# Centred queries and their exponentials in two PSUM banks, and another order of VectorE's work in a group of rows

## The chip, the cores and the metric

The kernel runs on one core of a Trainium2 chip. The metric is the device time of one launch in microseconds (us), the median of the runs shown. The core has five engines that work in parallel and meet only through semaphores: TensorE (PE in the profile, with its weight loads as PEld), VectorE (DVE), ScalarE (ACT), GpSimd (POOL), and SyncE (SP), which only issues transfers. Two memories matter here: SBUF, which all engines reach, and PSUM, eight banks of 128 partitions x 512 floats, into which TensorE writes.

## The reference, cut to what matters

```python
x = x + 0.5 * ffn(layernorm(x))        # mixture of 8 experts, top 2, with a capacity
x = x + attn(layernorm(x))
x = x + 0.5 * ffn(layernorm(x))

def attn(x):                           # x: 4 batches x 2048 rows x 256, 16 heads of 16 columns
    q = split_heads(x @ Wq + bq)
    v = split_heads(x @ Wv + bv)
    q = softmax(q, axis=-1) * s        # over the 16 columns of a head
    k = softmax(q, axis=-2) * s        # over the 2048 rows of a batch
    ctx = einsum('bhnd,bhne->bhde', k, v)
    return merge(einsum('bhnd,bhde->bhne', q, ctx)) @ Wo + bo
```

The change concerns the attention alone, and there the first softmax: subtract the maximum of a head, take the exponential, sum, divide.

## The kernel before, in words

The 8192 rows lie in SBUF as 64 tiles of 128 rows (`xs`). The attention works on groups of four tiles (a "quad", 512 rows); a batch has four of them, so there are 16. Each engine runs one function `body(b, j)` for batch b and step j; the order of the work on an engine is the order in which its `body` is written, and nothing reorders it. `quads(b, j)` returns the quads that a step handles in its different stages. In step (b, j), with s = j + 1: `far` is quad s+3 (VectorE takes its statistics), `ahead` is s+2 (ScalarE normalizes it, GpSimd takes the low half, SyncE transposes it with a transfer), `turned` is s+1 (TensorE computes the queries), `now` is s (the softmax), `past` is s-1 (TensorE accumulates the keys' products), and `done` is s-5, of the batch before (TensorE multiplies the transposed queries by the batch's small matrix, and VectorE adds the result to `xs`). Steps with b = -1 only fill the pipeline; batch 0 has no `done`; batches 1 and 2 run in a hardware loop; batch 3 has three steps and no `far`.

One quad passes through these pieces, by their names and the lines before:

- VectorE `stats` (L1182 to L1189): mean and variance of the four tiles. The variances go to 32 columns of PSUM bank 1 (`mv`). It waits for the transfer that loads the tiles. For batches 0 and 1 each quad has its own load. For batches 2 and 3 there are four loads of 1 MB, issued one in each step of batch 0, and `stats` of the first quad of batch 2, which is `far` in step (1, 0), waits until all of them have landed (`at.x1_in`, 16 * 2 * QUADS).
- GpSimd `power` (L468, L470), ScalarE `norm_x` (L778) and `norm_hi` (L786), GpSimd `norm_low` (L474), SyncE `turn_x` (L598): the normalized rows as two half-precision halves, transposed. SyncE issues the 1 MB load (L585) right behind `turn_x` in the same step.
- TensorE `queries` (L1484, L1486): into bank 2 (two tiles) and bank 3 (two tiles). It waits for `at.cent`, which says that VectorE has read those banks for the quad before.
- VectorE `center`: two reductions for the maxima of the heads (L1213), then two subtractions (L1217), from banks 2 and 3 into `qb`, a float32 buffer of 128 x 1024 in SBUF (it lies in the memory of `gat`, and goes by that name in the profile).
- ScalarE `queries_exp` (L790): one exponential over 1024 columns, in place in `qb`.
- VectorE `sum_heads` (L1223) and `soften` (L1228, L1229): sums of the heads, reciprocal, and one product of 1024 columns, in place in `qb`.
- ScalarE `keys_exp` (L797, L798) and `queries_hi` (L804), GpSimd `keys_low` (L484) and `queries_low` (L479): they read the softened `qb`. GpSimd's last one counts up `at.qlo`, which frees `qb` for the quad two later.
- TensorE `keys` (L1496, L1500) and `finish` (L1516, into banks 6 and 7), VectorE `finish` (L1198).

In step j = 0 of batches 1 to 3 the small matrix of the batch before is made, in a chain that goes back and forth between TensorE (`m2_ctx` L1525, `m2_out` L1533, `m2_turn` L1538, `m2_spread` L1542), VectorE (`m2_sums`, `m2_ctx` L1234, `m2_out` L1240 and L1243, `m2_top` L1247, `m2_scale`, `m2_lo` L1256) and ScalarE (`m2_hi` L808). TensorE's next `finish` waits for its end. Behind the last attention step the second expert block begins; GpSimd's first instruction of it, L418, stands in its queue behind `queries_low` of the last quad.

Of the kernel before, what the change touches and what calls it, by code (L numbers as in the profile page):

```python
# [6 lines left out]
def macaron_block(nc, x, wq, bq, wv, bv, wo, bo, router_w, wg, wu, wd, out):  # L7
    f32, f16, b16, i32, u32 = (mybir.dt.float32, mybir.dt.float16, mybir.dt.bfloat16,
                               mybir.dt.int32, mybir.dt.uint32)
    ALU, ACT, AX = mybir.AluOpType, mybir.ActivationFunctionType, mybir.AxisListType  # L10
    add, sub, mult = ALU.add, ALU.subtract, ALU.mult
# [3 lines left out]
    B, SEQ, D = x.shape  # L15
# [6 lines left out]
    H = 16  # L22
    DH = D // H
    HS = float((DH ** 0.5) ** -0.25)
    QTOP = 2.0 ** 14
    BT = SEQ // P
    QUADS = BT // 4
# [11 lines left out]
    EPS = 1e-5  # L39
    XSCALE = 2.0 ** 10  # L40
    WTOP = 13
    LOOP_STEPS = 56
    HSHIFT = 2.0 ** -39
    ROUNDS = 15
    ONE = 1 << 23
# [7 lines left out]
    with ctx:  # L53
# [43 lines left out]
        rws = sb("rws", [P, 8], f32)  # L97
# [73 lines left out]
        qmax, qsum = v1[:, :], v3[:, :]  # L171
# [103 lines left out]
        def bc(ap, axis, n):  # L275

            ap = ap.unsqueeze(axis)
            shape = list(ap.shape)
            shape[axis] = n
            return ap.to_broadcast(shape)  # L280
# [5 lines left out]
        def wait_for(eng, sm, n):  # L286

            if not (isinstance(n, int) and n <= 0):
                eng.wait_ge(sm, n)
# [32 lines left out]
        def in_batches(b):  # L322

            return not isinstance(b, int) or 0 <= b < B
# [333 lines left out]
        def _(act):  # L658
# [127 lines left out]
                act.activation(at_rows[j][:, :, 0:D], xn[:, r, :, :], ACT.Copy).then_inc(at.hi, 1)  # L786

            def queries_exp(b, j):
                act.wait_ge(at.cent, QUADS * b + j + 1)
                act.activation(qb[:, j % 2], qb[:, j % 2], ACT.Exp, scale=rws[:, 7:8]).then_inc(at.ex, 1)  # L790

            def keys_exp(b, j):
                q, r = QUADS * b + j, j % 2
# [54 lines left out]
        def _(dve):  # L848
# [352 lines left out]
            def by_head(ap):  # L1201
                return ap.rearrange("p (h d) -> p h d", d=DH)

            def heads_of(j):
                return qb[:, j % 2].rearrange("p t (h d) -> p (t h) d", d=DH)

            def center(b, j):

                q, q3 = QUADS * b + j, heads_of(j)
                part = [slice(k * 2 * H, (k + 1) * 2 * H) for k in range(2)]  # L1210
                for k in range(2):
                    dve.wait_ge(at.q, 2 * q + k + 1)
                    ch.mark(dve.tensor_reduce(qmax[:, part[k]], by_head(bank[2 + k][:, :]), AX.X, ALU.max))  # L1213
                ch.wait()
                wait_for(dve, at.qlo, q - 1)
                for k in range(2):
                    i = dve.tensor_tensor(q3[:, part[k]], by_head(bank[2 + k][:, :]), bc(qmax[:, part[k]], 2, DH), sub)  # L1217
                i.then_inc(at.cent, 1)

            def sum_heads(b, j):  # L1220

                dve.wait_ge(at.ex, QUADS * b + j + 1)
                ch.step(dve.tensor_reduce(qsum, heads_of(j), AX.X, add))  # L1223

            def soften(b, j):

                q3 = heads_of(j)
                ch.step(dve.reciprocal(qsum, qsum))  # L1228
                dve.scalar_tensor_tensor(q3, q3, HS * QTOP, bc(qsum, 2, DH), mult, mult).then_inc(at.qs, 1)  # L1229


            def m2_ctx(m):
# [30 lines left out]
            def body(b, steps):  # L1263
                for j in steps:
                    far, _, _, now, _, done = quads(b, j)
                    m = b - 1 if in_batches(b - 1) else None
                    if now:
                        center(*now)
                    if m is not None and j == 0:
                        m2_sums(m)  # L1270
                        m2_ctx(m)
                        m2_out(m)
                    if far:
                        stats(*far)
                    if m is not None and j == 0:
                        m2_top(m)
                    if done and j == 1:
                        finish(done[0], 0)
                    if now:
                        sum_heads(*now)  # L1280
                    if m is not None and j == 0:
                        m2_scale(m)
                    if now:
                        soften(*now)
                    if m is not None and j == 0:
                        m2_lo(m)
                    if done and j:
                        finish(*done)

            def looped(b, steps):  # L1290
# [30 lines left out]
        def _(pe):  # L1321
# [153 lines left out]

            def queries(b, j, k):
                q = QUADS * b + j
                wait_for(pe, at.cent, q)
                if k == 0:
                    pe.wait_ge(xt_in[j % 2], turned_by((b, j)))  # L1480
                for t in range(2):
                    for n, (a, w) in enumerate(HALVES):
                        for d in range(KD):
                            i = pe.matmul(bank[2 + k][:, t * D:(t + 1) * D], at_xt[j % 2][:, 2 * k + t, a * KD + d, :],  # L1484
                                          wq16[:, w, d, :], start=(n == 0 and d == 0), stop=False)
                    i = pe.matmul(bank[2 + k][:, t * D:(t + 1) * D], bq_one[:, :], bq16[:, :], start=False, stop=True)  # L1486
                i.then_inc(at.q, 1)
# [95 lines left out]
            ffn(sems[0], 0, nothing)  # L1583
            attention_start()
            batches(pe, body)
            pe.wait_ge(at.cent, B * QUADS)
            attention_end(-1)
            ffn(sems[1], 3, attention_end)

# [22 lines left out]
```

## Time and profile before

| | us |
|---|---|
| median of 3 runs | 1919.36 |
| lowest and highest run | 1918.79 and 1923.34 |
| the profiled execution, by the clock of the other runs | 1917.76 |
| its span in the profile | 1916.0 |
| TensorE busy | 1616.2 |
| VectorE busy | 1246.2 |
| ScalarE busy | 887.6 |
| GpSimd busy | 874.8 |

The attention lies from about 857 to 1062 us of the span. The busy times are sums over the whole kernel, most of which is the two expert blocks, where TensorE is busy nearly all the time; they say little of the attention. There the timeline of each engine is read: each row has its start, the time that it took, the engine, the line, the operation, what is written and read, how many instructions are merged in the row, and in brackets how long the engine was idle before it and what released it.

### The profile page before, as it was taken

What the parts mean: (1) busy time and instruction counts of PE and PEld (TensorE: products, weight loads), DVE (VectorE), ACT (ScalarE), POOL (GpSimd) and SP (SyncE); (2) the same over time, 40 slices, a digit from 0 to 9 for tenths busy, and PEclk for the clock granted to TensorE, in tenths of its full rate; (3) what the DMA queues carried; (4) which work ended last, traced back from release to release, by engine and by line L of the source; (5) the groups of instructions that cost most, each with busy time, mean ns of one, the idle gap of its engine ahead of it and who ended that gap; (6) DMA issues with size and microseconds to landing.
All of it is one profiled execution on the core that took longest, in us unless ns stands there. A gap on an engine that the chain in (4) does not pass through costs nothing.

```text
span 1916.0 us, 40317 instructions
## 1 busy us (share of the span) xinstructions
PE 1616.2 (84%) x13943; PEld 1275.8 (67%) x13943; DVE 1246.2 (65%) x2883; ACT 887.6 (46%) x1627; POOL 874.8 (46%) x636
## 2 busy tenths in 40 slices
PE   4512899999999999995899751289999999999998
PEld 3411687877878787773577641168787787878876
DVE  8987748576574856526898897763745546465551
ACT  4511445445454444535665551144544545445452
POOL 5623262644536354235776652326264452635423
PEclk9999999999999999996999755589999999999999
DMA  6650461614425152226766450045161442515212
GB/s 214 212 185 14 108 122 30 145 41 107 78 70 126 37 132 52 31 29 165 154 146 146 137 195 4 14 108 116 36 145 44 104 83 65 128 42 126 58 25 28
DMA packets 261236, 182.16 MB, mean 95 GB/s; under 512 B 160938, under 2 KB 247860, under 8 KB 261172
## 3 DMA queue, kind: packets, MB, share of 16 engines
q1 hardware_dynamic: 230452, 139.37, 26.7%
q0 software_dynamic: 30720, 41.96, 13.2%
q8 instruction: 36, 0.59, 0.1%
q14 instruction: 28, 0.23, 0.0%
HBM read 89.01 MB, written 54.53 MB: 75 GB/s over the span
## 4 chain that ended last, share of the span: by engine, by line
PE 72%; DVE 12%; issue 6%; POOL 5%; DMA 2%; ACT 2%; DVEq 0%; SPq 0%; POOLq 0%; ACTq 0%
PE bank L1439 43%; PE bank L1452 22%; PE bank L1420 3%; POOL rstd L418 1%; POOL rows L422 1%; DVE kT L1020 1%; DVE rT L1020 1%; PE bank L1400 1%; DVE gat L1229 1%; PE bank L1484 1%; ACT xn L778 1%; DMA xs<-in_L_attn_x 1%; POOL gat L395 1%; DVE xn L937 1%; DVE v L1223 1%
## 5 line engine op out<-in xcount | busy, mean ns | idle before, releaser
L1439 PE MATMUL bank<-xT,w_g 128*128 128x320 f16 x3072 | 503.1, 300 | 30.9 <-DMA xT<-gat 30.9
L1095 DVE SCALAR_TENSOR_TENSOR unit_buf<-bank,sc_cur,unit_buf 128x320 f32<-128x320 f32 x512 | 281.5, 550 | 353.9 <-PE bank L1439 227.9
L1439 PE MATMUL bank<-xT,w_u 128*128 128x320 f16 x3072 | 502.5, 300 | 0.0
L720 ACT ACTIVATE unit_buf<-bank,sc_cur 128x320 f32<-128x320 f32 x512 | 269.5, 526 | 407.1 <-PE bank L1439 405.6
L1452 PE MATMUL bank<-w_d,xs 128*128 128x256 f16 x3840 | 423.8, 273 | 0.0
L1452 PEld LDWEIGHTS bank<-w_d,xs 128*128 128x128 f16 x3840 | 375.2, 98 | 44.4
L1439 PEld LDWEIGHTS bank<-xT,w_g 128*128 128x128 f16 x3072 | 295.7, 99 | 141.0 <-issue 30.6
L389 POOL TENSOR_TENSOR hot_v<-hot_b,val 128x400 bf16<-128x400 bf16 x128 | 147.7, 1154 | 519.9 <-DVE hot_b L1078 519.9
L1439 PEld LDWEIGHTS bank<-xT,w_u 128*128 128x128 f16 x3072 | 301.3, 98 | 117.7
L1101 DVE TENSOR_TENSOR xs<-unit_buf,xs 128x320 f16<-128x320 f32 x512 | 268.0, 523 | 2.2
L395 POOL DMA_INDIRECT gat<-rows_d,id_next x160 | 177.0, 1106 | 200.4 <-DVE id_next L1088 140.0
L726 ACT ACTIVATE xs<-unit_buf 128x320 f16<-128x320 f32 x512 | 235.8, 461 | 10.4 <-DVE unit_buf L1095 10.4
L745 ACT ACTIVATE xs<-bank,w_fac 128x256 f32<-128x256 f32 x160 | 76.0, 475 | 277.4 <-PE bank L1452 276.3
L408 POOL DMA_INDIRECT out_x<-xs,id_cur x80 | 143.0, 1788 | 84.6 <-issue 76.1
L408 POOL DMA_INDIRECT x_d<-xs,id_cur x80 | 142.6, 1782 | 84.0 <-issue 73.6
L915 DVE SCALAR_TENSOR_TENSOR w_g<-raw_gu,sc_next,w_g 128x1024 f16<-128x1024 f32 x32 | 41.1, 1284 | 93.2 <-ACT w_g L661 93.2
L1420 PEld LDWEIGHTS bank<-hot_v,hot_a 128*128 128x128 bf16 x1024 | 82.3, 161 | 28.5 <-DVE hot_a L1080 24.3
L1420 PE MATMUL bank<-hot_v,hot_a 128*128 128x50 bf16 x1024 | 80.6, 219 | 22.2 <-POOL hot_v L389 22.2
L1400 PE MATMUL bank<-cnt,same_e 128*128 128x3 f32 x60 | 17.6, 363 | 95.7 <-DVE rT L1020 95.7
L422 POOL TENSOR_TENSOR rows<-xn,rows 128x1024 f16<-128x1024 f32 x32 | 68.4, 2136 | 45.2 <-ACT rows L667 45.2
L1080 DVE TENSOR_TENSOR hot_a<-pos_a,slot_a 128x1024 bf16<-128x1024 bf16 x128 | 87.3, 682 | 0.0
L1400 PEld LDWEIGHTS bank<-cnt,same_e 128*128 128x128 f32 x60 | 15.0, 310 | 98.9 <-DVE rT L1020 98.9
(229 smaller groups left out, 1815.2 us busy)
## 6 DMA issues: line engine op xcount, KB each, us to landing
rows_d<-rows SPq DMA_DIRECT2D x32, 512.0 KB, 3.4
raw_gu<-in_L_ffn_wg SPq DMA_DIRECT2D x16, 1024.0 KB, 6.3
raw_gu<-in_L_ffn_wu SPq DMA_DIRECT2D x16, 1024.0 KB, 9.3
raw_d<-in_L_ffn_wd SPq DMA_DIRECT2D x16, 1024.0 KB, 5.5
x_d<-xs SPq DMA_DIRECT2D x1, 8192.0 KB, 32.6
out_x<-xs SPq DMA_DIRECT2D x16, 512.0 KB, 3.7
xs<-in_L_attn_x SPq DMA_DIRECT2D x7, 1024.0 KB, 5.6
xs<-x_d SPq DMA_DIRECT2D x5, 1024.0 KB, 6.1
```

The source lines that it names most:

```text
L389: pool.tensor_tensor(hot_v[:, r], bc(hot_b[:, r], 2, 5), bc(vv, 3, ST), mult).then_inc(S.hot_v_ready, 1)
L395: pool.indirect_dma_start(out=gat[:, s, :], out_offset=None, in_=rows_d, in_offset=bass.IndirectOffsetOnAxis(ap=id_next[:, s:s + 1], axis= ...
L408: pool.indirect_dma_start(out=dst, out_offset=bass.IndirectOffsetOnAxis(ap=id_cur[:, s:s + 1], axis=0), in_=stage[:, s, :], in_offset=None ...
L422: pool.tensor_tensor(rows[:, r, :, D:2 * D], xn[:, r, :, :], rows[:, r, :, 0:D], sub).then_inc(S.lo_ready, 1)
L720: act.activation(act_s[:, u % 2, :], bank[u % 2][:, 0:CW], ACT.Silu, scale=sc_cur[:, 3:4]).then_inc(S.s_ready, 1)
L726: act.activation(hid[:, 0, f, c * CW:(c + 1) * CW], h32[:, u % HB, :], ACT.Copy).then_inc(S.hhi_ready, 1)
L1080: dve.tensor_tensor(hot_a[:, r], bc(pa, 1, P), slot_a[:, :, :], ALU.is_equal).then_inc(S.hot_a_ready, 1)
L1095: dve.scalar_tensor_tensor(h32[:, u % HB, :], bank[2 + u % 2][:, 0:CW], sc_cur[:, 4:5], act_s[:, u % 2, :], mult, mult).then_inc(S.h32_rea ...
L1101: dve.tensor_tensor(hid[:, 1, f, c * CW:(c + 1) * CW], h32[:, u % HB, :], hid[:, 0, f, c * CW:(c + 1) * CW], sub).then_inc(S.h_ready, 1)
L1420: last = pe.matmul(bank[6][:, 0:5 * ST], hot_a[:, i % 2, :, t], hot_v[:, i % 2, t].rearrange("p v s -> p (v s)"), start=(i == 0 and t == 0 ...
L1439: mm = pe.matmul(bank[2 * m + u % 2][:, 0:CW], wgu[m][:, w, k, f * P:(f + 1) * P], xT[:, a * KD + k, c * CW:(c + 1) * CW], start=(j == 0 a ...
L1452: mm = pe.matmul(bank[4 + s % 2][:, 0:D], hid[:, a, f, s * P:(s + 1) * P], wdn[:, w, f, :], start=(f == 0 and j == 0), stop=(f == FT - 1 a ...
```

## The change

`center` now writes its differences into PSUM banks 0 and 1 (which the attention did not use otherwise, but for the 32 columns of `mv` in bank 1), the exponential runs there in place, in two instructions of 512 columns, the sums of the heads are taken from there in two, and `soften` reads the banks and writes `qb` in two. The wait for `at.qlo` moves from `center` to `soften`. `at.cent` and `at.ex` count two per quad, and `queries` waits for each of its banks alone. In VectorE's `body`, `stats` moves ahead of `center`, and `finish` of steps j > 1 moves from the end of the step to the place between `center` and `sum_heads`.

```diff
             def queries_exp(b, j):
-                act.wait_ge(at.cent, QUADS * b + j + 1)
-                act.activation(qb[:, j % 2], qb[:, j % 2], ACT.Exp, scale=rws[:, 7:8]).then_inc(at.ex, 1)
+                q = QUADS * b + j
+                for k in range(2):
+                    act.wait_ge(at.cent, 2 * q + k + 1)
+                    act.activation(bank[k][:, :], bank[k][:, :], ACT.Exp, scale=rws[:, 7:8]).then_inc(at.ex, 1)
...
             def center(b, j):
...
                 ch.wait()
+                for k in range(2):
+                    dve.tensor_tensor(by_head(bank[k][:, :]), by_head(bank[2 + k][:, :]), bc(qmax[:, part[k]], 2, DH),
+                                      sub).then_inc(at.cent, 1)
+
+            def sum_heads(b, j):
+
+                q = QUADS * b + j
+                for k in range(2):
+                    dve.wait_ge(at.ex, 2 * q + k + 1)
+                    ch.mark(dve.tensor_reduce(qsum[:, part[k]], by_head(bank[k][:, :]), AX.X, add))
+                ch.wait()
+
+            def soften(b, j):
+
+                q = QUADS * b + j
+                ch.step(dve.reciprocal(qsum, qsum))
                 wait_for(dve, at.qlo, q - 1)
                 for k in range(2):
-                    i = dve.tensor_tensor(q3[:, part[k]], by_head(bank[2 + k][:, :]), bc(qmax[:, part[k]], 2, DH), sub)
-                i.then_inc(at.cent, 1)
-
-            def sum_heads(b, j):
-
-                dve.wait_ge(at.ex, QUADS * b + j + 1)
-                ch.step(dve.tensor_reduce(qsum, heads_of(j), AX.X, add))
-
-            def soften(b, j):
-
-                q3 = heads_of(j)
-                ch.step(dve.reciprocal(qsum, qsum))
-                dve.scalar_tensor_tensor(q3, q3, HS * QTOP, bc(qsum, 2, DH), mult, mult).then_inc(at.qs, 1)
+                    last = dve.scalar_tensor_tensor(by_head(qb[:, j % 2, 2 * k:2 * k + 2].rearrange("p t d -> p (t d)")),
+                                                    by_head(bank[k][:, :]), HS * QTOP, bc(qsum[:, part[k]], 2, DH),
+                                                    mult, mult)
+                last.then_inc(at.qs, 1)
...
                     m = b - 1 if in_batches(b - 1) else None
+                    if far:
+                        stats(*far)
                     if now:
                         center(*now)
                     if m is not None and j == 0:
                         m2_sums(m)
                         m2_ctx(m)
                         m2_out(m)
-                    if far:
-                        stats(*far)
+                    if done and j > 1:
+                        finish(*done)
                     if m is not None and j == 0:
                         m2_top(m)
                     if done and j == 1:
...
                         m2_lo(m)
-                    if done and j:
+                    if done and j == 1:
                         finish(*done)
...
             def queries(b, j, k):
                 q = QUADS * b + j
-                wait_for(pe, at.cent, q)
+                wait_for(pe, at.cent, 2 * q - 1 + k)
```

The first place is VectorE's queue at step (1, 0), behind the branch into the loop (L299). In the rows `v` stands for the small buffers of maxima and sums, `gat` for `qb`, `bst` for the statistics, `zr`, `wT`, `t` and `mx` for pieces of the small matrix. Before:

```order
L299 UNCONDITIONAL_BRANCH
L1213 TENSOR_REDUCE v<-bank 128x32 [waits at_q]
L1217 TENSOR_TENSOR gat<-bank,v 128x512 [waits at_qlo,at_dstep]
L1260 RECIPROCAL zr<-bank 128x2 [waits at_gt]
L1234 TENSOR_TENSOR wT<-bank,same_h 128x256 [waits at_ctx]
L1240 SCALAR_TENSOR_TENSOR t<-bank,zr,rT 128x256 [waits at_a]
L1243 TENSOR_REDUCE mx<-t 128x1 [waits at_dstep]
L289 ISA [waits at_x1_in]
L1182 BN_STATS bst<-xs 128x6
L1247 TENSOR_REDUCE m_top_s<-bank 1x1 [waits at_m_max]
L1223 TENSOR_REDUCE v<-gat 128x64 [waits at_ex]
```

The same place now; L1184 is `stats`, L1216 the subtraction, L1224 the sums.

```order
L299 UNCONDITIONAL_BRANCH
L289 ISA [waits at_x1_in]
L1184 BN_STATS bst<-xs 128x6
L1213 TENSOR_REDUCE v<-bank 128x32 [waits at_q]
L1216 TENSOR_TENSOR bank<-bank,v 128x512 [waits at_dstep]
L1267 RECIPROCAL zr<-bank 128x2 [waits at_gt]
L1241 TENSOR_TENSOR wT<-bank,same_h 128x256 [waits at_ctx]
L1247 SCALAR_TENSOR_TENSOR t<-bank,zr,rT 128x256 [waits at_a]
L1250 TENSOR_REDUCE mx<-t 128x1 [waits at_dstep]
L1254 TENSOR_REDUCE m_top_s<-bank 1x1 [waits at_m_max]
L1224 TENSOR_REDUCE v<-bank 128x32 [waits at_ex] x2
```

The statistics, and with them the wait for the loads (`at_x1_in`), have moved from behind `m2_out` to the head of the step, ahead of the centring and of the whole chain for the small matrix.

The second place is VectorE's queue in step j = 2 of the loop; L1198 (now L1200) is `finish`. Before:

```order
L1223 TENSOR_REDUCE v<-gat 128x64 [waits at_ex]
L1228 RECIPROCAL v<-v 128x64 [waits at_dstep]
L1229 SCALAR_TENSOR_TENSOR gat<-gat,v 128x1024 [waits at_dstep]
L1198 ISA [waits at_out]
L1198 SCALAR_TENSOR_TENSOR xs<-bank,mx,xs 128x512
```

And now, from the subtraction on:

```order
L1216 TENSOR_TENSOR bank<-bank,v 128x512
L1197 ISA
L1200 ISA [waits at_out]
L1200 SCALAR_TENSOR_TENSOR xs<-bank,mx,xs 128x512
L1224 TENSOR_REDUCE v<-bank 128x32 [waits at_ex] x2
L1230 RECIPROCAL v<-v 128x64 [waits at_dstep]
L1233 SCALAR_TENSOR_TENSOR gat<-bank,v 128x512 [waits at_qlo,at_dstep]
```

The additions to `xs`, which wait for TensorE's product (`at_out`), have moved ahead of the sums and of the softening.

## Rows read from the trace of the kernel before

**Rows 1.** By stretch: length, busy PE, PEld, DVE, ACT, POOL (count), PEclk, DMA share, GB/s.
```profile
922.77:932.99 10.22, 7.37 (x57) 4.61 (x53) 8.55 (x18) 6.90 (x9) 8.49 (x6) 0.83 1.05 208
948.25:993.01 44.76, 41.15 (x383) 31.96 (x384) 41.32 (x90) 28.92 (x39) 33.01 (x20) 1.00 0.68 144
```
**Rows 2.** Timeline of VectorE, one step of batch 0: start, duration, then the instruction.
```profile
912.56 1.27 DVE L1213 TENSOR_REDUCE v<-bank 128x32 f32<-128x512 f32 x2
913.87 1.29 DVE L1217 TENSOR_TENSOR gat<-bank,v 128x512 f32<-128x512 f32 x2
915.07 1.39 DVE L1182 BATCH_NORM_STATS2 bst<-xs 128x6 f32<-128x256 f32 x4
...
918.65 1.22 DVE L1223 TENSOR_REDUCE v<-gat 128x64 f32<-128x1024 f32 x1 [1.38 <-ACT gat L790]
...
920.49 2.35 DVE L1229 SCALAR_TENSOR_TENSOR gat<-gat,v 128x1024 f32<-128x1024 f32 x1
```
**Rows 3.** Timeline of ScalarE, the same step.
```profile
912.67 1.06 ACT L797 ACTIVATE xT<-gat 128x1024 f32<-128x1024 f32 x1 [3.32 <-DVE gat L1229]
...
915.52 2.06 ACT L778 ACTIVATE xn<-xs,nmean,rstd 128x256 f32<-128x256 f32 x4
917.49 1.13 ACT L790 ACTIVATE gat<-gat,rws 128x1024 f32<-128x1024 f32 x1
```
**Rows 4.** Timelines of GpSimd and VectorE, where L1229 and GpSimd meet and where not.
```profile
919.64 2.13 POOL L474 TENSOR_TENSOR rows<-xn,rows 128x1024 f16<-128x1024 f32 x1 [0.67 <-ACT rows L786]
921.73 1.99 POOL L468 TENSOR_TENSOR rstd<-rstd,mhalf 128x4 f32<-128x4 f32 x1
...
943.75 1.01 POOL L468 TENSOR_TENSOR rstd<-rstd,mhalf 128x4 f32<-128x4 f32 x1
946.22 1.23 DVE L1229 SCALAR_TENSOR_TENSOR gat<-gat,v 128x1024 f32<-128x1024 f32 x1
```
**Rows 5.** Groups by line, VectorE, 892 to 1036 us: count | busy, mean ns | idle.
```profile
L1217 DVE TENSOR_TENSOR gat<-bank,v 128x512 f32<-128x512 f32 x26 | 16.7, 686 | 0.4
L1198 DVE SCALAR_TENSOR_TENSOR xs<-bank,mx,xs 128x512 f32 x16 | 11.2, 738 | 0.2
```
**Rows 6.** Timelines of ScalarE, SyncE and VectorE around the last load of batches 2 and 3.
```profile
927.70 1.13 ACT L790 ACTIVATE gat<-gat,rws 128x1024 f32<-128x1024 f32 x1
934.09 1.05 SPq L585 DMA_DIRECT2D xs<-x_d  x1
941.18 1.40 DVE L1182 BATCH_NORM_STATS2 bst<-xs 128x6 f32 x4
```
**Rows 7.** Columns as in rows 1: the two microseconds in which the transfers end.
```profile
939.00:940.00 1.00, 1.00 (x8) 0.78 (x8) 0.33 (x1) 1.00 (x3) 0.84 (x1) 1.00 0.48 169
940.00:941.00 1.00, 1.00 (x10) 0.59 (x7) 0.97 (x3) 1.00 (x2) 0.00 (x0) 1.00 0.00 0
```
**Rows 8.** Timeline of TensorE, first `finish` behind step (1, 0).
```profile
948.25 2.79 PE L1516 MATMUL bank<-kT,raw_gu 128*128 128x256 f16 x24 [1.14 <-DVE kT L1256]
```
**Rows 9.** Chain that ended last, step (3, 0), without statistics: start, duration, what.
```profile
1027.75 1.13 PE bank L1533 x4
...
1035.53 0.75 DVE kT L1256
```
**Rows 10.** Timeline of TensorE: queries after a long idle time, and without one.
```profile
878.66 1.46 PE L1484 MATMUL bank<-wq,xt 128*128 128x256 f16 x6 [15.90 <-DMA xt<-rows]
...
950.87 0.82 PE L1484 MATMUL bank<-wq,w_u 128*128 128x256 f16 x6
```
**Rows 11.** Timelines of TensorE, VectorE and GpSimd at the end of the attention.
```profile
1048.49 2.78 PE L1516 MATMUL bank<-kT,raw_gu 128*128 128x256 f16 x24
...
1046.45 1.28 DVE L1213 TENSOR_REDUCE v<-bank 128x32 f32<-128x512 f32 x2
...
1052.11 1.23 DVE L1229 SCALAR_TENSOR_TENSOR gat<-gat,v 128x1024 f32<-128x1024 f32 x1
...
1059.62 1.98 POOL L418 TENSOR_TENSOR rstd<-rstd,mhalf 128x4 f32<-128x4 f32 x2
```

More of the change, by code:

```diff
@@ L41, in macaron_block @@
     WTOP = 13
-    LOOP_STEPS = 56
+    LOOP_STEPS = 60
     HSHIFT = 2.0 ** -39
@@ L1202, in by_head @@
                 return ap.rearrange("p (h d) -> p h d", d=DH)
-            def heads_of(j):
-                return qb[:, j % 2].rearrange("p t (h d) -> p (t h) d", d=DH)
+            part = [slice(k * 2 * H, (k + 1) * 2 * H) for k in range(2)]
             def center(b, j):
-                q, q3 = QUADS * b + j, heads_of(j)
-                part = [slice(k * 2 * H, (k + 1) * 2 * H) for k in range(2)]
+                q = QUADS * b + j
                 for k in range(2):
@@ L1214, in center @@
                 ch.wait()
+                for k in range(2):
[8 more added lines that the diff above has]
+            def soften(b, j):
+                q = QUADS * b + j
+                ch.step(dve.reciprocal(qsum, qsum))
                 wait_for(dve, at.qlo, q - 1)
                 for k in range(2):
-                    i = dve.tensor_tensor(q3[:, part[k]], by_head(bank[2 + k][:, :]), bc(qmax[:, part[k]], 2, DH), sub)
-                i.then_inc(at.cent, 1)
-            def sum_heads(b, j):
-                dve.wait_ge(at.ex, QUADS * b + j + 1)
-                ch.step(dve.tensor_reduce(qsum, heads_of(j), AX.X, add))
-            def soften(b, j):
-                q3 = heads_of(j)
-                ch.step(dve.reciprocal(qsum, qsum))
-                dve.scalar_tensor_tensor(q3, q3, HS * QTOP, bc(qsum, 2, DH), mult, mult).then_inc(at.qs, 1)
+                    last = dve.scalar_tensor_tensor(by_head(qb[:, j % 2, 2 * k:2 * k + 2].rearrange("p t d -> p (t d)")),
+                                                    by_head(bank[k][:, :]), HS * QTOP, bc(qsum[:, part[k]], 2, DH),
+                                                    mult, mult)
+                last.then_inc(at.qs, 1)
             def m2_ctx(m):
@@ L1585, in _ @@
             batches(pe, body)
-            pe.wait_ge(at.cent, B * QUADS)
+            pe.wait_ge(at.cent, 2 * B * QUADS)
             attention_end(-1)
```

## The prediction, made before the changed kernel ran

> **What bounds the kernel now.** I read the page first: TensorE is busy for most of the span, but in the expert blocks, which the change doesn't touch. So the question is what sets the pace in the attention, from 857 to 1062 us, and the view for it is the busy time by stretch, then the timelines of single engines there. The reader is to see two regimes. In batch 0 a step takes 10.2 us and no engine is full: TensorE 7.4, VectorE 8.6, ScalarE 6.9, GpSimd 8.5 [rows 1]. Such a pace is set by a ring of waits. From batch 1 on a batch of four steps takes 44.76 us, with TensorE busy for 41.15 and VectorE for 41.32: there the two are nearly full, and a cut in waiting can bring 3.6 us a batch at most [rows 1].
>
> The ring of batch 0 reads off two timelines. ScalarE's L797 starts when VectorE's L1229 has ended (it waited 3.32 us for it); from its start at 912.67 ScalarE goes without a gap through L797, L798, L804 and L778 to the exponential, which starts at 917.49 and ends at 918.62 [rows 3]. VectorE, idle for 1.38 us, starts the sums at 918.65, and L1229 at 920.49; it ends at 922.84, which frees ScalarE again [rows 2]. Around: 4.82 to the exponential, 1.13 in it, 1.84 for sums and reciprocal, 2.35 for L1229, some 0.07 of hand-over: 10.21.
>
> L1229 takes 1.23 us where GpSimd isn't at work on SBUF, and 2.35 in the ring; there GpSimd's L474 runs from 919.64 to 921.77, and 921.77 plus 1.1 is just where L1229 ends. The other way round GpSimd's tiny L468 takes 1.99 beside L1229 and 1.01 away from it [rows 2, 4]. Both are one at a time: each costs the other about 1 us. VectorE's L1217 and L1198, with one operand in PSUM and one large or small one in SBUF, keep their means of 686 and 738 ns over 892 to 1036 us, though GpSimd works most of that time [rows 1, 5].
>
> [...]
>
> **The change, part by part.**
>
> *The ring in batch 0.* The product reads PSUM. I take 2 x 0.67 = 1.35 us for its two halves, between L1217 and L1198, which have its form [rows 5]; bounds 1.25 and 1.5. The two exponentials of 512 columns: L790 takes 1.13 for 1024, so a half has about 0.43 of columns and 0.2 to 0.25 of fixed time; both take 1.2 to 1.3 [rows 3]. No row has an activation that reads and writes PSUM; at worst 0.1 more each. But VectorE starts its first sum after the first half, so behind the second only a half sum, 0.64, stands, and the reciprocal, 0.6. The new ring: 4.82 + 1.3 + 0.7 + 0.6 + 1.35 + 0.03 = 8.8 us, against 10.21. VectorE needs for itself 2.05 (statistics, with their waits) + 2.56 (centring, L1213 and L1217 [rows 2]) + 1.3 + 0.55 + 1.35 = 7.8, and GpSimd, rid of its own 1 us, 7.6. The transfers are the tight resource: 1.05 of 10.22 us in the row of the last step [rows 1], with overlaps counted twice. I let them take 0.3 us back in all. In the first quad the 2.05 us of statistics no longer stand between centring and sums, but in idle time ahead of the queries; the exponentials' 1.3 and their hand-overs remain there, and I estimate 0.45 from it. Four turns of the ring lie between the exponential of quad 0 and that of quad 4: 4 x 1.41 + 0.45 - 0.3 = **-5.8 us** (bounds -3.1, if transfers hold a step at 9.55, and -7.2).
>
> [...] The rows show 1.27 for two reductions of 512 from PSUM against 1.22 for one of 1024 from SBUF, 0.05 apart; my sum goes by these.
>
> *The wait for the last load.* In step (1, 0), `stats` needs the last 1 MB load of batches 2 and 3. SyncE issues it at 934.09, 5.3 us after the end of the exponential of quad 4 (928.83), behind the transposition that follows that exponential. Transfers still run to the middle of 939 to 940 and then stop; so the load lands near 940.1, 11.3 us after the exponential [rows 6, 7]. Before, VectorE softened, centred and made the small matrix first, came to `stats` at 941.18 and didn't wait. Now `stats` is first. VectorE has softened 2.6 us after the exponential and stands there for 8.7 us. Behind it in its queue are the centring (TensorE's next queries wait for that), the sums, and the chain for the small matrix, for which `finish` waits. From the landing: stats 2.05, centring 2.56, masked product 0.85, 0.1 to TensorE's `m2_out`. From there to the end of L1256 the rows of step (3, 0), where VectorE has no statistics in between, as now, give 1036.28 - 1027.75 = 8.5 us; 0.2 more for the halves, 8.7 [rows 9]. Then TensorE's clock: it is idle for some 8 us ahead of this. After an idle time of 15.9 us it worked at 1.2 instead of 2.4 GHz (six matmuls in 1.46 instead of 0.82 us) [rows 10]. I take 2.2 us, bounds 0 and 5. Sum: 11.3 + 2.05 + 2.56 + 0.85 + 0.1 + 8.7 + 2.2 = 27.8 us from the exponential to the first `finish`, against 948.25 - 928.83 = 19.4 before [rows 6, 8]: **+8.4 us** (bounds +5.5 and +12).
>
> *Batches 1 and 2.* L1229 no longer stretches, and `finish` covers the exponential. VectorE's own order, all starts added: step j = 1 10.5, j = 2 and 3 9.2 each, then stats, centring and masked product 5.5, and 8.7: 43.1 us with hand-overs, against 44.76. **-1.65 us.** From `finish` of batch 1 to that of batch 2 there are no stats in the last step, but TensorE's products of the keys end only then; I count -0.9 there. Together -2.55 (bounds 0, if TensorE sets the pace with its waits, and -5, if both batches come down to 42.3).
>
> *The end.* In the last step VectorE centres from 1046.45 to 1049.05; `finish` now stands ahead of the sums, and TensorE ends that product only at 1048.49 + 2.78 = 1051.27. So VectorE waits for TensorE: 1052.0 behind `finish`, then 1.3 + 0.55 + 1.35 = 1055.2, where L1229 ended at 1053.34 before. Behind it are ScalarE's and GpSimd's last pieces, and GpSimd's L418, which opened the second expert block at 1059.62 [rows 11]. **+1.8 us** (bounds 0 and 2.6).
>
> The wait moved to `soften` is for quad q-2 and long fulfilled. The column range of `mv` in bank 1 meets no instruction of another engine. `queries` gets bank 2 some 0.6 us earlier, hidden. The rest of the kernel is the same.
>
> Sum: -5.8 + 8.4 - 2.55 + 1.8 = +1.85 us. The profiled execution took 1917.76 (span 1916.0), so 1919.6 there. The median of the runs shown is 1.6 higher, 1919.36, so **1921.2 us**.
>
> **The rivals.**
>
> *The load isn't missed.* If it lands by the time VectorE comes to it, or with little wait (the sooner transposition and a load that needs fewer than 6 us would do it), the path from exponential to `finish` is bound by TensorE's keys and `m2_ctx`, and comes to about 18.5 us instead of 27.8: 0.9 below the 19.4. The sum is then -5.8 - 0.9 - 2.55 + 1.8 = -7.5: **1911.9 us**, faster. For it: the load's landing is inferred from the transfers' activity, not shown. Against it: 5.3 us to the issue are the same chain as before, and VectorE arrives at 2.6.
>
> *VectorE waits for TensorE in each `finish`.* By my schedule VectorE reaches `finish` in steps 2 and 3 about 15.0 and 24.2 us behind the first one, and TensorE has its products at 14.8 and 24.3. There is no slack. It decides when TensorE is more than 0.2 us later, as behind a late transposition or at the low clock; then each of the four steps loses what TensorE is late, say 1.2, and the saving of the two batches turns into a loss: +4.8 over my sum, **1926.0 us**, slower. Against it: TensorE has 3.6 us of idle time a batch to catch up in [rows 1].
>
> *The contention stays.* If an input in PSUM doesn't free the product from GpSimd, about 1.1 us return in each of 8 steps, and GpSimd keeps its 1.99: +9, **1930 us**. Against it stands L1217 [rows 5].
>
> **How the numbers follow.** Forecast 0.62, load not missed 0.15, `finish` waits 0.17, contention stays 0.06. The forecast's own range is 1916 to 1926. Taking in most of the first two rivals, the range is 1913 to 1928. A change of this kernel can be told from none beyond 0.3%, 5.8 us: faster means below 1913.6, slower above 1925.1. The forecast gives some 0.08 of its chance to slower and 0.02 to faster; the first rival is mostly faster, the second and third mostly slower: faster 0.15, same 0.62, slower 0.23.
>
> **What would show it.** Right, if: in batch 0 a step takes 8.7 to 9.1 us; the product's halves take 0.65 to 0.7 us each beside GpSimd's L474, and L468 takes 1.01; in step (1, 0) VectorE is idle for 7 to 10 us ahead of its first statistics, released by a transfer, and TensorE works at a lower clock right behind; the two batches take 42 to 43.5 us each; and VectorE's last `finish` waits some 2 us for TensorE. Wrong, if that idle time is under 3 us, if batch 0 keeps 10.2 us a step, or if VectorE waits for TensorE in every `finish` of the loop.

## The result, and the profile after

| | before | after |
|---|---|---|
| median of 6 runs each, us | 1919.45 | 1928.51 |
| lowest to highest | 1918.79 to 1923.34 | 1928.01 to 1929.17 |
| ratio, 95% interval | | 1.0043 (1.0033 to 1.0054) |
| profiled execution, its span | 1917.76, 1916.0 | 1928.49, 1926.8 |

The changed kernel is slower by 9.1 us. The forecast was 1921.2, with a range of 1913 to 1928: the median lies 0.5 us above the range's upper end, and the case that came true, slower, had 0.23. The ratio is that of the two kernels' runs with its interval; the medians of the table give 1.0047.

The attention can be measured by itself, from VectorE's write of `same_h` (859.88 before, 859.97 after) to GpSimd's L418 (1059.62 [rows 11], and 1068.67). It took 199.74 us before and takes 208.70 after: 8.96 more, nearly the whole difference of the medians. The landmarks between are the end of the exponential of quad 4 and TensorE's first `finish` product of each batch.

| stretch, us | before | after | change | predicted |
|---|---|---|---|---|
| to the exponential of quad 4 | 68.95 | 63.02 | -5.9 | -5.8 |
| from there to the first finish | 19.42 | 29.12 | +9.7 | +8.4 |
| batch 1, finish to finish | 44.76 | 47.18 | +2.4 | -1.65 |
| batch 2 | 43.32 | 43.81 | +0.5 | -0.9 |
| to L418 | 23.29 | 25.57 | +2.3 | +1.8 |

**The ring.** VectorE's timeline of one step of batch 0 after the change (start, duration, instruction), which answers to [rows 2]:

```profile
893.77 1.30 DVE L1216 TENSOR_TENSOR bank<-bank,v 128x512 f32<-128x512 f32 x2
895.94 1.29 DVE L1224 TENSOR_REDUCE v<-bank 128x32 f32<-128x512 f32 x2 [0.87 <-ACT bank L792]
897.26 0.55 DVE L1230 RECIPROCAL v<-v 128x64 f32<-128x64 f32 x1
897.85 1.29 DVE L1233 SCALAR_TENSOR_TENSOR gat<-bank,v 128x512 f32<-128x512 f32 x2
```

And GpSimd's, beside it, for [rows 4]:

```profile
897.54 2.13 POOL L474 TENSOR_TENSOR w_g<-xn,w_g 128x1024 f16<-128x1024 f32 x1 [0.80 <-ACT w_g L786]
899.62 1.01 POOL L468 TENSOR_TENSOR rstd<-rstd,mhalf 128x4 f32<-128x4 f32 x1
```

L1233's two halves take 1.29 together in the middle of L474, where one instruction took 2.35, and L468 is back at 1.01. Of the four steps between the exponentials of quads 0 and 4 three take 8.7 us and one 9.1.

**The load.** VectorE and SyncE in step (1, 0), which answer to [rows 6]:

```profile
924.37 1.29 DVE L1233 SCALAR_TENSOR_TENSOR gat<-bank,v 128x512 f32<-128x512 f32 x2
936.34 1.40 DVE L1184 BATCH_NORM_STATS2 bst<-xs 128x6 f32 x4 [10.68 <-DMA xs<-x_d]
```

```profile
923.42 4.61 SPq L607 DMA_TRANSPOSE raw_gu<-unit_buf  x1
928.21 2.02 SPq L598 DMA_TRANSPOSE xt<-w_g  x1
930.27 0.89 SPq L585 DMA_DIRECT2D xs<-x_d  x1
```

VectorE stands for 10.68 us. The load is issued 7.3 us after the exponential (its end is 922.99) instead of 5.3, because SyncE needs 4.61 us for the transposition ahead of it, L607, for which it needed 1.95 before:

```profile
929.33 1.95 SPq L607 DMA_TRANSPOSE raw_gu<-unit_buf  x1
```

It comes back in split_again and ahead_end, below, with 4.51 and 4.40 us at the same place. Behind the wait TensorE's timeline:

```profile
941.82 2.07 PE L1542 MATMUL bank<-wo,wT 128*128 128x256 f32 x4 [10.03 <-DVE wT L1241]
943.68 1.49 PE L1493 MATMUL bank<-wq,xt 128*128 128x256 f16 x6
...
952.11 2.79 PE L1525 MATMUL bank<-kT,raw_gu 128*128 128x256 f16 x24 [0.41 <-DVE kT L1263]
956.07 0.83 PE L1493 MATMUL bank<-wq,w_u 128*128 128x256 f16 x6 [1.17 <-DVE bank L1216]
```

It worked at the lower level, 1.2 GHz, right behind 10 us of idling (the granted clock is 0.50 from 940 to 944 us): six matmuls in 1.49 us, in 0.83 later.

**The batches.** The last row shows the first of two surprises, in step 1. Before, VectorE centred right behind the end of the small matrix, and TensorE had the free banks when its first `finish` product was done. Now the statistics stand between them, and TensorE waits 1.17 us. Step 1 has two `finish`es, that of quad 0 ahead of the sums and that of quad 1 at its end; VectorE waits in both halves of the second, and the step takes 11.8 us from centring to centring (954.00 to 965.80), where the prediction counted 10.5:

```profile
961.71 0.75 DVE L1200 SCALAR_TENSOR_TENSOR xs<-bank,mx,xs 128x512 f32 x1 [0.69 <-PE bank L1525]
963.02 0.75 DVE L1200 SCALAR_TENSOR_TENSOR xs<-bank,mx,xs 128x512 f32 x1 [0.56 <-PE bank L1525]
```

The second surprise stands in step (2, 0). First VectorE, then GpSimd, then TensorE:

```profile
986.60 0.16 DVE L1267 RECIPROCAL zr<-bank 128x2 f32<-128x2 f32 x1
986.80 1.81 DVE L1268 TENSOR_SCALAR zr<-zr 128x2 f32<-128x2 f32 x1
```

```profile
986.46 2.12 POOL L479 TENSOR_TENSOR unit_buf<-gat,unit_buf 128x1024 f16<-128x1024 f32 x1 [0.18 <-ACT unit_buf L806]
```

```profile
989.07 1.50 PE L1542 MATMUL bank<-wo,wT 128*128 128x256 f32 x4 [2.34 <-DVE wT L1241]
990.36 1.48 PE L1493 MATMUL bank<-wq,xt 128*128 128x256 f16 x6
```

L1268 scales two numbers per partition, from SBUF to SBUF. It ends at 988.61, L479 at 988.58: it took until GpSimd's instruction was done. TensorE's idle time ahead of `m2_out` is 2.34 us, against 0.66 in the same step before, and behind it the clock is low again for a while (0.61 from 989 to 992 us). The two stretches after, for [rows 1] (columns as there):

```profile
952.11:999.29 47.18, 42.48 (x383) 32.48 (x384) 40.74 (x98) 29.48 (x43) 30.06 (x20) 0.96 0.65 134
999.29:1043.10 43.81, 40.93 (x384) 31.92 (x385) 38.39 (x88) 29.43 (x43) 28.91 (x18) 1.00 0.64 141
```

**The end.** VectorE waits for TensorE in the last early `finish`, as [rows 11] had it coming, by 1.04 and 0.92 us:

```profile
1056.87 0.75 DVE L1200 SCALAR_TENSOR_TENSOR xs<-bank,mx,xs 128x512 f32<-128x512 f32 x1 [1.04 <-PE bank L1525]
1058.54 0.75 DVE L1200 SCALAR_TENSOR_TENSOR xs<-bank,mx,xs 128x512 f32<-128x512 f32 x1 [0.92 <-PE bank L1525]
...
1061.11 1.29 DVE L1233 SCALAR_TENSOR_TENSOR gat<-bank,v 128x512 f32<-128x512 f32 x2
```

### The profile page after: what moved, and what is told of

Its sections match the earlier page's. It is cut to its first block, busy times and chain, and to the rows that moved or that the text cites. A ratio compares the mean times of both kernels' runs of the same rounds, so it can differ in the third digit from the quotient of the medians.

```text
span 1926.8 us, 40369 instructions
## 1 busy us (share of the span) xinstructions
PE 1614.3 (84%) x13943; PEld 1274.2 (66%) x13943; DVE 1242.0 (64%) x2915; ACT 889.2 (46%) x1643; POOL 864.2 (45%) x636
## 3 DMA queue, kind: packets, MB, share of 16 engines
q0 software_dynamic: 30720, 41.96, 13.3%
## 4 chain that ended last, share of the span: by engine, by line
PE 75%; DVE 10%; issue 5%; POOL 4%; DMA 3%; ACT 1%; SPq 1%; DVEq 0%; POOLq 0%; ACTq 0%
PE bank L1448 43%; PE bank L1461 22%; PE bank L1429 3%; PE bank L1493 2%; PE bank L1525 1%; POOL rstd L418 1%; PE bank L1505 1%; DVE kT L1022 1%; DVE rT L1022 1%; POOL rows L422 1%; PE bank L1409 1%; DMA xs<-in_L_attn_x 1%; DVE xn L939 1%; PE bank L1495 1%; POOL hot_v L389 1%
## 5 line engine op out<-in xcount | busy, mean ns | idle before, releaser
L395 POOL DMA_INDIRECT gat<-rows_d,id_next x160 | 180.9, 1130 | 200.4 <-DVE id_next L1090 140.0
L408 POOL DMA_INDIRECT out_x<-xs,id_cur x80 | 138.9, 1737 | 84.6 <-issue 76.1
```

The source lines that it names most:

```text
L395: pool.indirect_dma_start(out=gat[:, s, :], out_offset=None, in_=rows_d, in_offset=bass.IndirectOffsetOnAxis(ap=id_next[:, s:s + 1], axis= ...
L408: pool.indirect_dma_start(out=dst, out_offset=bass.IndirectOffsetOnAxis(ap=id_cur[:, s:s + 1], axis=0), in_=stage[:, s, :], in_offset=None ...
```

## The experiments

All runs in one table. Stretches in us, each from one trace, "first finish" from the write of `same_h`, the others as above; "ratio" compares the run with before on the same chip, and can differ by up to 0.0014 from the quotient of the medians. split_wait, stats_back, psum_only and order_only ran on a chip on which before takes 2008.57 us (the block ahead of the attention is some 40 us slower there). The three of these with the PSUM banks have ratios 0.0034 to 0.0051 below those of their near twins split_again, back_odd and move_odd. The attention of stats_back and psum_only is within 1 us of their twins', and split_wait's is even 4.3 us longer than split_again's. Why is open, since before has no trace on that chip; the text below leans on their stretches alone.

| kernel | first finish | batch 1 | batch 2 | end | attention | ratio (95%) |
|---|---|---|---|---|---|---|
| before | 88.37 | 44.76 | 43.32 | 23.29 | 199.7 | 1 |
| before_again | 88.59 | 45.46 | 44.71 | 23.29 | 202.1 | |
| after | 92.14 | 47.18 | 43.81 | 25.57 | 208.7 | 1.0043 (1.0033, 1.0054) |
| split_wait | 84.64 | 48.21 | 43.79 | 25.23 | 201.9 | 0.9938 (0.9917, 0.9960) |
| split_again | 83.77 | 44.76 | 43.79 | 25.24 | 197.6 | 0.9989 (0.9980, 0.9997) |
| stats_back | 87.86 | 47.27 | 47.23 | 25.60 | 208.0 | 1.0010 (0.9995, 1.0025) |
| back_odd | 89.20 | 47.28 | 47.25 | 25.24 | 209.0 | 1.0044 (1.0031, 1.0057) |
| psum_only | 87.70 | 45.52 | 42.45 | 22.37 | 198.0 | 0.9942 (0.9925, 0.9958) |
| move_odd | 87.48 | 45.46 | 42.44 | 22.36 | 197.7 | 0.9988 (0.9980, 0.9997) |
| order_only | 96.07 | 50.64 | 45.76 | 25.10 | 217.6 | 1.0098 (1.0081, 1.0116) |
| ahead_end | 81.68 | 47.09 | 43.79 | 22.37 | 194.9 | 0.9975 (0.9967, 0.9984) |
| ahead_end_zr | 84.95 | 44.77 | 43.80 | 22.37 | 195.9 | 0.9965 (0.9952, 0.9977) |
| best | 82.54 | 44.16 | 43.44 | 22.36 | 192.5 | 0.9948 (0.9935, 0.9961) |
| sbuf_best | 89.98 | 52.28 | 47.54 | 23.28 | 213.1 | 1.0054 (1.0040, 1.0067) |

before_again is before once more, for its trace:

> The kernel before, unchanged, for its trace on the same chip as the variants. I measure the attention's length from VectorE's write of same_h to GpSimd's L418 of the second expert block: 199.7 us in the first trace of before. If the attention doesn't depend on the chip it is 199.2 to 200.2 here, and all differences of whole runs between variants beyond their attention's lengths are noise of the expert blocks; if this chip's transfers are slower, it is above 203, and the variants' gains over before are larger here than on the first chip.

Its attention came out 2.3 us longer than in the first trace, above what I expected. In steps (2, 0) and (3, 0) TensorE's matmuls fell into the lower clock (`m2_out` took 1.82 and 2.08 us instead of 1.12 and 1.13), and 2.1 of the 2.3 us lie in the two batches that end there. So 2 us between two single traces of the attention is noise, and a smaller difference needs the ratio or the row that makes it.

**The wait for the loads.** split_wait, and the same kernel again as split_again:

```diff
-                elif j == 0:
-                    dve.wait_ge(at.x1_in, 16 * 2 * QUADS)
+                elif j % 2 == 0:
+                    dve.wait_ge(at.x1_in, 16 * (QUADS + 1 + j // 2) + 32 * (b - 2))
```

> The changed kernel, but the statistics of a quad of batches 2 and 3 wait only for the load that holds that quad, not for all four. Theory (the wait for the last load costs most of the loss): VectorE no longer waits in step (1, 0), and TensorE's first finish comes 9 to 11 us sooner, bound by the keys and m2_ctx (exponential of quad 4 to finish about 18.5 us instead of 29); everything behind keeps its pace, 47 and 44 us for the two batches. Total 1928.5 - 10 = 1918.5 us (1917 to 1920.5). Rival (other engines give it back, because transfers or TensorE are just as late): less than 3 us of gain, 1926 or more.

> The same kernel as split_wait (the changed kernel, with VectorE's statistics waiting for their own load alone), on a chip where the kernel before takes the 1919 us of the first trace, since on the other chip transfers and expert blocks took longer. Theory A (the wait for all loads is worth 6 to 8 us): no idle time of VectorE ahead of the statistics in step (1, 0), the first finish at 82 to 85 us instead of 92.1, batches as in the changed kernel (47.2 and 43.8) and the end too, so the attention is 200 to 203 us long and the run 6 to 8 us below the changed kernel's 1928.5: 1920.5 to 1922.5. Theory B (VectorE then waits for something else there, for the low clock's matmuls or for TensorE): the first finish above 88, the run above 1925.

VectorE no longer idles there, and the first `finish` comes at 83.8 us instead of 92.1: 8.4 us for the wait. It is one trace; the other kernels with the same banks, order up to there and own-load wait (split_wait, ahead_end, ahead_end_zr, best) have it at 81.7 to 85.0, so the wait is worth 7 to 10 us. split_again's median is 1917.82, 10.7 below after's, more than expected, since L1268 this time met no GpSimd instruction in batch 1. Its rows, and the stretch of that batch:

```profile
978.71 0.17 DVE L1268 TENSOR_SCALAR zr<-zr 128x2 f32<-128x2 f32 x1
1021.74 1.25 DVE L1268 TENSOR_SCALAR zr<-zr 128x2 f32<-128x2 f32 x1
```

```profile
944.02:988.78 44.76, 41.07 (x383) 31.83 (x384) 39.22 (x98) 29.49 (x43) 30.07 (x20) 1.00 0.70 142
```

In the table batch 1 takes 44.8 us where L1268 took 0.17 and 47.1 to 48.2 where it took 1.49 or 1.81 (after, ahead_end, split_wait), all with the same order in that batch's steps 0 and 1. In batch 2 the stretch costs nothing: L1268 took 1.25 or 1.26 us in after, split_wait and split_again and 0.24 in ahead_end, and the batch takes 43.8 us in all four. There TensorE's product ends only behind L1268, and VectorE waits for it in any case: 0.46 us more in after, 1.47 in ahead_end.

**The order's two parts, undone one by one.** In stats_back and psum_only the statistics stand behind the small matrix again. Mean and variance can't then lie in bank 1, where the exponentials are, so they went to a small buffer in SBUF:

```diff
-                    ch.mark(dve.bn_aggr(mv[:, r, g, :], bst[:, r, g, :]))
+                    ch.mark(dve.bn_aggr(at_mv[:, r, g, :], bst[:, r, g, :]))
...
-                dve.tensor_scalar(nmean[:, r, :], mv[:, r, :, 0], -1.0, None, mult)
+                dve.tensor_scalar(nmean[:, r, :], at_mv[:, r, :, 0], -1.0, None, mult)
```

> The changed kernel with the statistics back in their old place, behind m2_out; since bank 1 is in use there, mean and variance go to a small SBUF buffer instead. Theory (statistics ahead of the centring cost the load wait, and in the loop hold back TensorE's queries in step 1 and the small matrix in step 0): the load wait is gone (-10), the two batches take about 43.5 and 42.5 us instead of 47.1 and 43.9 (-5): 1913.5 us (1911 to 1916). Rival (the loop is slow for another reason, the stretched L1268 and TensorE waits in finish): batches stay at 46 to 47 and 44, 1918 to 1919. If the two small operations on the new SBUF buffer get into the way of GpSimd, they take 1 to 2 us instead of 0.16 in many steps and the total is up to 8 us more.

> Only the move to PSUM: all of VectorE's work in the order of before, mean and variance in a small SBUF buffer as in stats_back. Theory: finish ahead of the sums isn't needed where the statistics cover the exponential, and it costs about 2 us at the end of the attention, so this is 0 to 3 us faster than stats_back: 1911.5 us (1909 to 1915). Batch 0 keeps its 8.8 us a step. Rival (the early finish helps, as cover): slower than stats_back by 1 us or more.

> Only VectorE's new order (statistics first, finish in the middle for j > 1), with the centred queries in SBUF as before. Theory (the order loses, PSUM wins): batch 0 keeps 10.2 us a step, in step (1, 0) VectorE waits 6 to 9 us for the load, and the loop loses too: 1919.4 + 8 + 5 + 2 = 1934 us (1930 to 1938). Rival (the move to PSUM is what costs): about 1919 to 1922 us.

order_only shows the reorder without the move: 17.8 us more attention, with a wait of 7.42 us for the load. The other two missed what was expected of them: the wait for the load is gone in both, but stats_back's batches take 47.3 and 47.2 us instead of 43.5 and 42.5, and psum_only's attention is only 1.7 us shorter than before's. They were confounded by that buffer (L1191, `nmean` from it, takes up to 2.03 us), so they were run again with five columns in it instead of four:

> The move to PSUM with the order of before, and mean and variance in SBUF with five columns instead of four (one of padding), so that VectorE's two small instructions on them have an odd width. Theory A: what stretched those instructions to 0.65 to 1.96 us in psum_only is that VectorE takes a fast mode for an even number of elements from SBUF to SBUF and must wait for GpSimd there. Then with five columns each takes 0.16 us, the steps of batch 0 take 8.7 to 8.9 us instead of 9.5, a batch takes 42.8 to 43.3 us instead of 45.5 (1.14 + 0.49 + 0.48 + 0.55 less), and the attention 187 to 191 us against 198.0. Theory B: any VectorE instruction from SBUF to SBUF waits, whatever its width; then all stays as in psum_only, 197 to 199.

> The same, but with finish of steps j > 1 between the centring and the sums, as in the changed kernel. Theory A (the early finish is what costs the batches): VectorE comes to it before TensorE has the product, waits there 1 to 2.5 us in each of those steps and holds up the sums behind it: batches longer than move_odd's by 1.5 to 2.5 us each, the end by 2 to 2.5 us, the attention 6 to 9 us longer than in move_odd. Theory B (only the place of the statistics costs the batches): the attention is at most 2.5 us longer than in move_odd, all of it at the end.

Theory A of move_odd fell: the odd width changes nothing. A group of VectorE's instructions by form, 880 to 1060 us, and one of them with GpSimd's instruction beside it:

```profile
L1192 DVE TENSOR_SCALAR nmean<-at_mv 128x5 f32<-128x5 f32 x13 | 15.3, 1177 | 0.4
```

```profile
897.86 1.96 DVE L1192 TENSOR_SCALAR nmean<-at_mv 128x5 f32<-128x5 f32 x1
899.73 0.16 DVE L1193 TENSOR_SCALAR rstd<-at_mv 128x5 f32<-128x5 f32 x1
```

```profile
897.67 2.12 POOL L480 TENSOR_TENSOR unit_buf<-gat,unit_buf 128x1024 f16<-128x1024 f32 x1
```

L1192 ends at 899.82, L480 at 899.79. Read from PSUM the same operation takes 0.16. With that cost in it, the move with the old order still gives 0.9988, and `finish` made early on top of it 1.0044: 11.2 us more attention, of which 2.9 are the end, 6.6 the two batches, and the rest lies ahead of the first `finish`, where the two kernels are the same. In back_odd's step 3 L1192 takes 1.96 us (0.64 in move_odd) and the scaling behind it 1.64 (0.31), TensorE idles 3.0 us in both batches and falls to the lower clock. I put the batches' length down to that chain, and not to a wait in `finish`, since VectorE doesn't wait for TensorE in the loop's `finish` there at all; no run has the early `finish` with that buffer and without the stretch. Theory A had the cost but not its place.

ahead_end is split_again with `finish` of every step back at the step's end:

```diff
-                    if done and j > 1:
-                        finish(*done)
...
-                    if done and j == 1:
+                    if done and j:
                         finish(*done)
```

> split_wait (the changed kernel with statistics waiting for their own load alone) with finish of all steps put back at the end of the step; the statistics stay ahead of the centring. Against split_wait's 201.9 us. Theory A (both parts of the order cost): the end gets back 2 to 2.5 us and the steps 2 and 3 of the batches some 0.5 us each, but step 1 keeps TensorE waiting for the centring (1.2 us of TensorE idle ahead of the queries, VectorE 1.2 us late in finish): 196 to 199 us, still 4 or more above move_odd. Theory B (only the early finish costs): within 1.5 us of move_odd.

The end comes down from 25.24 to 22.37, and batch 2 stays at 43.79; batch 1 is 2.3 us longer, which is L1268 again (1.49 us here, 0.17 in split_again). With the statistics ahead, the early `finish` costs 2.9 us, at the end alone. The run is 4.2 us below before.

**L1268.** ahead_end_zr scales first, from PSUM, and takes the reciprocal in SBUF:

```diff
-                ch.step(dve.reciprocal(zr[:, :], bank[5][:, 0:KD]))
-                ch.mark(dve.tensor_scalar(zr[:, :], zr[:, :], HS, None, mult))
+                ch.step(dve.tensor_scalar(zr[:, :], bank[5][:, 0:KD], 1.0 / HS, None, mult))
+                ch.mark(dve.reciprocal(zr[:, :], zr[:, :]))
```

> ahead_end with the scaling of the sums' reciprocal in another order: the tensor_scalar reads PSUM (bank 5, times 1/HS) and the reciprocal of 128 x 2 then runs in SBUF. Theory A (a tensor_scalar with input and output in SBUF waits for GpSimd's instruction, one from PSUM doesn't, and a reciprocal doesn't): L1267 and L1268 take 0.16 to 0.17 us each in every batch, where L1268 took 1.49; TensorE waits 1.2 us less for the masked product and keeps its clock; batch 1 gets 1.3 to 2.5 us shorter (47.1 to 44.6 to 45.8), batch 2 stays at 43.8, the run 1912.5 to 1914. Theory B (what is stretched is whichever small instruction stands there): the new instruction from PSUM takes 1.4 us and nothing changes, 1915.

All eight instructions take 0.15 to 0.17 us, and batch 1 takes 44.77 us instead of 47.09. In that batch no GpSimd instruction happened to run at that place. In batch 2 GpSimd's L484 ran over both, and they still took 0.16 and 0.17; in batch 1 it is best, below, that has one there. VectorE and GpSimd in best:

```profile
976.76 0.15 DVE L1267 TENSOR_SCALAR zr<-bank 128x2 f32<-128x2 f32 x1
976.95 0.17 DVE L1268 RECIPROCAL zr<-zr 128x2 f32<-128x2 f32 x1
```

```profile
976.06 2.12 POOL L479 TENSOR_TENSOR unit_buf<-gat,unit_buf 128x1024 f16<-128x1024 f32 x1 [0.93 <-ACT unit_buf L806]
```

The median of ahead_end_zr fell by 1.4 us, inside the two intervals; the attention doesn't show it as a whole, because the first `finish` came 3.3 us later (TensorE waited 2.68 us for transposed rows instead of 1.46, and VectorE then for it).

**Step 1.** best puts the statistics of step j = 1 behind its softening:

```diff
-                    if far:
+                    if far and j != 1:
                         stats(*far)
...
+                    if far and j == 1:
+                        stats(*far)
                     if done and j:
```

> ahead_end_zr, with the statistics of step j = 1 put behind that step's softening, so that the centring, which frees TensorE's banks, comes first behind m2_lo there. Theory A (the centring behind the statistics is what holds TensorE in step 1): TensorE doesn't wait 1.17 us for L1216 behind its first finish, VectorE doesn't wait 0.7 and 0.55 us for the second finish, and each of the batches 1 and 2 gets 1.2 to 2 us shorter: 42.3 to 43.5 each, the run 1909 to 1912. Theory B (the time comes back, because ScalarE now waits for those statistics in step 2 and its exponentials come late): the batches stay within 0.5 us of ahead_end_zr's.

TensorE goes from `finish` to the queries without a gap. The gain is 0.6 and 0.35 us in the batches, half or less of what I expected at the least: VectorE now idles 0.93 us ahead of the sums, and TensorE 0.8 us one step later, as Theory B had it in part. best takes 1910.19 us, 9.8 below before on its chip and 18.3 below the changed kernel.

**The move alone, under the best order.** sbuf_best is best with queries and exponentials in SBUF again, as in before:

> The order, the wait and the scaling of best, with queries and exponentials in SBUF as in the kernel before. It says what the PSUM banks are worth by themselves. Theory A (the move frees VectorE's product and GpSimd from each other, and this is a gain of its own): the steps of batch 0 take 10.2 us again instead of 8.7, which alone is 5.9 us to the fourth exponential, and in the batches the product takes 2.35 us in some steps: each 0.5 to 2 us longer; the attention 199 to 203 us against best's 192.5, the run 1917 to 1921. Theory B (the order gives the gain, and the product's contention is hidden in it): the run within 2 us of best's 1910.2.

It takes 1931.03, 20.8 us more than best, twice what Theory A said. VectorE's timeline in a step of batch 1, and GpSimd's:

```profile
968.47 1.22 DVE L1223 TENSOR_REDUCE v<-gat 128x64 f32<-128x1024 f32 x1 [1.22 <-ACT gat L790]
969.73 0.55 DVE L1228 RECIPROCAL v<-v 128x64 f32<-128x64 f32 x1
970.32 2.36 DVE L1229 SCALAR_TENSOR_TENSOR gat<-gat,v 128x1024 f32<-128x1024 f32 x1
```

```profile
969.47 2.12 POOL L474 TENSOR_TENSOR rows<-xn,rows 128x1024 f16<-128x1024 f32 x1 [3.10 <-ACT rows L786]
971.55 1.99 POOL L468 TENSOR_TENSOR rstd<-rstd,mhalf 128x4 f32<-128x4 f32 x1
```

In SBUF the order of before is the better one: sbuf_best has 13.3 us more attention than before, though it also has the loads' own wait and the other scaling. In steps 1 to 3 of batch 1 VectorE idles 1.43, 1.22 and 1.21 us ahead of the sums, where the statistics of before's order left 0, 0.49 and 0; TensorE idles 2.83 us for the centring of step 2 and 2.88 us ahead of `m2_out`, and its clock is low behind that. L1229 takes 2.36 us in steps 1 to 3, in before 1.65 and twice 2.36.

In PSUM no run shows which order is better. best has 5.2 us less attention than move_odd, but 4.9 of these lie ahead of the first `finish`, where move_odd's L1192 takes 1.96 us and its steps 9.5 instead of 8.7; the two batches take 87.6 us in best and 87.9 in move_odd. The old order in PSUM, with mean and variance out of the way of GpSimd, was not run.

## Why the prediction was right or wrong

- **The ring, -5.8:** right in size and cause. Steps of 8.8 us were forecast and 8.7 measured, but for one of 9.1, and the halves take 0.65 us each. The sum reads rows 1 loosely in one place: their 1.05 is a share of the time and not microseconds.
- **The wait for the last load, +8.4:** right in mechanism, 1.3 too small. The idle time is 10.7 us, not 8.7: the load landed 13.3 us after the exponential, where 11.3 was carried over from before. I took SyncE's queue as unchanged, but its L607 takes 4.61 us to issue where it took 1.95. The transfers are closer together now, which may be why; no run tests it. From the landing on it was 0.7 shorter than counted. split_again prices the wait at 8.4 us, within 7 to 10.
- **Batches 1 and 2, -2.55:** the step that failed; +2.9 in its place, 5.4 of the 7.3 us by which the forecast was low. The size of the loss is uncertain, since before's second trace has 90.2 us for the two batches and its first 88.1; but the forecast 85.5 is missed in all three traces with this order, after, split_wait and split_again (91.0, 92.0 and 88.6). I added VectorE's own instructions and took TensorE as following. Steps 2 and 3 came as counted (9.05 and 9.2). Step 1 took 11.8 instead of 10.5, because moving the centring behind the statistics also moves what TensorE waits for; the prediction called that move only for step (1, 0). Step 0 of the next batch took 17.1, where 14.2 was left for it: L1268 held up beside GpSimd, and TensorE's low clock behind; split_again, where L1268 met nothing, has a batch 1 that is 2.4 us shorter. The variants with the other scaling and with the other step 1 took back 2.3 and 1.0 us over both batches, and even best needs 44.2 and 43.4, not 43.1 and 42.4: the sum of starts on one engine is a lower bound.
- **The end, +1.8:** right in mechanism; it took +2.3, since VectorE starts the second half 0.5 us after TensorE's product ends (1058.03, and 1058.54), which the sum put at nothing. Putting it back gains 2.9.
- **The rivals.** The load was missed, and the contention of the product is gone. The second rival gave a number (1926.0) nearer to the result than my sum, but not by its mechanism: in the loop VectorE waits for TensorE only in the second `finish` of step 1, not in steps 2 and 3. Of the signs, the one that failed is that of the batches, 42 to 43.5 us each.
- **The chances.** A sum of +1.85 with bounds that were lopsided upwards (a wait of unknown length, a low clock) deserved more than 0.23 on slower.

## What to carry to other kernels

Moving an instruction to the head of a queue moves its waits ahead of everything, so look first at the widest condition behind its semaphore; here one constant (all loads instead of its own) cost some 8 us, nearly the whole loss. An order is good only together with the durations that it covers: this one by itself, in SBUF, cost 17.8 us, so run the change and the order each alone. And of a chain that goes back and forth between engines, read every link's duration, the tiny ones too: one of 0.17 us took 1.81 and cost 2.3 in one batch, and took 1.26 and cost nothing in the next, where another wait covered it.

## What the hardware showed beside

A VectorE `tensor_scalar` from SBUF to SBUF on 128x2, 128x4 or 128x5 elements takes 0.16 us alone, and up to 2.03 us beside a GpSimd instruction of 128x1024. Over the 14 traces, from 860 to 1110 us, 77 of them start inside such an instruction with at least 0.15 us of it left, and all 77 end 0.02 to 0.04 us behind its end; what counts is how much of it is left, and not their own size. The same from PSUM takes 0.15 or 0.16 us there in all 252 cases, a reciprocal of 128x2 in SBUF takes 0.17 (six cases), and the aggregation from SBUF to SBUF (move_odd's L1190) at most 0.18 in 52. The trace of before has L1261 at 1.03, 0.32 and 0.33 us; the prediction weighed contention for the large product alone and passed over it. The Trainium skill, SBUF — State Buffer, "Who interferes with whom", lists `tensor_scalar` among the instructions that can take the port shared with GpSimd; and VectorE: DVE Perf Modes, "Mode 2×_2P — use both read ports for one tensor", allows that mode for an even count, or for an odd one equal in source and destination, which fits what move_odd ran into. The runs agree with both as far as they go: they show who waits and until when, and not the mode.
